# Shared experts' norms without a mean: centred down weights, routed rows centred on their way out of PSUM, variances in 32 rows

## The reference

```python
m = jnp.mean(x, axis=-1); v = jnp.var(x, axis=-1); norm = (x - m) / jnp.sqrt(v + 1e-5)
# 8 experts of 352 hidden features, the best 2 of them for each token
y = jnp.einsum('tef,te,ehf->th', act, combine, down_weights)
# shared expert of 704 hidden features, for every token
y = y + (silu(x @ gate.T) * (x @ up.T)) @ shared_down.T
x = norm(x + y)
```

## Time and profile before

| | us |
|---|---|
| median of 3 runs (2693.25 to 2711.85) | 2700.85 |
| the profiled execution, its own time | 2698.7 |
| its span in the profile | 2696.9 |
| TensorE busy in the span | 2416.9 (90%) |
| VectorE busy | 1855.0 (69%) |
| GpSimd busy | 1347.0 (50%) |
| ScalarE busy | 1281.6 (48%) |

### The profile page before, as it was taken

The page is one execution under the profiler, slowest core; times in us unless marked ns, Lnnn a source line. Parts: engine busy times, 40 slices in busy tenths (PEclk is TensorE's granted clock), DMA queues, the critical chain, the costliest instruction groups (busy, mean ns, idle before and its releaser), DMA issues.

```text
span 2696.9 us, 33625 instructions
## 1 busy us (share of the span) xinstructions
PE 2416.9 (90%) x11898; PEld 1391.1 (52%) x11898; DVE 1855.0 (69%) x2248; ACT 1281.6 (48%) x2059; POOL 1347.0 (50%) x610
## 2 busy tenths in 40 slices
PE   7887749999999999999488899999999988999998
PEld 2333324444677999865133333333433333678886
DVE  5768875544665666575799889889988988741222
ACT  4444335531234666443657656764675452234433
POOL 0222239850050000340699999999999995122221
PEclk9999869989899999999799899999999999999999
DMA  6464443332064777540464675666577555100000
GB/s 231 144 156 112 127 104 93 91 101 94 13 231 143 271 269 271 196 152 18 127 194 160 188 213 175 201 194 195 172 198 215 195 180 204 45 1 16 1 16 32
DMA packets 251641, 387.11 MB, mean 144 GB/s; under 512 B 131776, under 2 KB 154304, under 8 KB 243808
## 3 DMA queue, kind: packets, MB, share of 16 engines
q1 hardware_dynamic: 232016, 336.76, 38.5%
q0 software_dynamic: 9296, 38.80, 5.8%
q10 hardware_dynamic: 10176, 9.50, 1.0%
HBM read 315.00 MB, written 62.65 MB: 140 GB/s over the span
## 4 chain that ended last, share of the span: by engine, by line
PE 56%; DVE 13%; POOL 10%; issue 9%; DMA 5%; ACT 4%; SPq 2%; ACTq 0%; PEldq 0%; PEld 0%; POOLq 0%; DVEq 0%
PE psum L2143 8%; POOL arena L862 5%; PE psum L2090 5%; PE psum L2324 4%; PE psum L2325 4%; POOL arena L854 3%; DMA arena<-bc_scr 3%; PE psum L3235 2%; PE psum L3035 2%; DVE arena L2787 2%; SPq L2417 2%; PE psum L2297 2%; PE psum L1986 2%; PE psum L2298 2%; PE psum L1988 2%
## 5 line engine op out<-in xcount | busy, mean ns | idle before, releaser
L854 POOL TENSOR_TENSOR arena<-arena 128x2048 f32<-128x2048 f32 x128 | 600.8, 4694 | 111.0 <-DVE arena L1635 74.7
L2143 PE MATMUL psum<-arena,cst 128*128 128x512 f32 x1024 | 501.8, 625 | 92.9 <-POOL arena L862 83.1
L1162 ACT ACTIVATE psum<-arena,negA 128x512 f32<-128x512 f32 x512 | 333.4, 682 | 281.1 <-DVE arena L1650 240.4
L2143 PEld LDWEIGHTS psum<-arena,cst 128*128 128x128 f32 x1024 | 188.4, 195 | 385.6 <-issue 209.8
L1650 DVE TENSOR_TENSOR_SCAN arena<-psum,arena 128x512 f32<-128x512 f32 x256 | 310.8, 1214 | 101.6 <-POOL arena L854 58.8
L862 POOL TENSOR_TENSOR arena<-arena 128x1024 f32<-128x1024 f32 x128 | 323.3, 2526 | 19.3 <-DMA arena<-bc_scr 10.3
L1650 DVE TENSOR_TENSOR_SCAN psum<-psum,arena 128x512 f32<-128x512 f32 x256 | 296.9, 1205 | 0.1
L911 POOL TENSOR_TENSOR arena<-arena 128x512 f32<-128x512 f32 x64 | 87.1, 1361 | 324.8 <-ACT arena L1286 319.3
L2090 PE MATMUL psum<-arena 128*128 128x512 f32 x512 | 231.5, 596 | 1.3 <-PE psum L2090 0.8
L1770 DVE TENSOR_TENSOR r<-arena,r 128x512 fp32r<-128x512 f32 x64 | 46.1, 722 | 237.6 <-ACT r L1291 237.5
L2324 PE MATMUL psum<-r 128*128 128x512 f32 x512 | 201.5, 394 | 3.6 <-ACT arena L1286 2.5
(11 more groups left out here) (392 smaller groups left out, 4868.5 us busy)
## 6 DMA issues: line engine op xcount, KB each, us to landing
arena<-bc_scr SPq DMA_DIRECT2D x256, 512.0 KB, 4.8
arena<-w_exp SPq DMA_DIRECT2D x23, 1408.0 KB, 6.1
arena<-in_gu SPq DMA_DIRECT2D x44, 512.0 KB, 4.8
arena<-in_inw SPq DMA_DIRECT2D x32, 512.0 KB, 3.5
arena<-in_dn SPq DMA_DIRECT2D x31, 512.0 KB, 6.9
x_scr<-arena SPq DMA_DIRECT2D x19, 512.0 KB, 6.0
arena<-in_x SPq DMA_DIRECT2D x8, 1024.0 KB, 10.1
w_exp<-in_gu SPq DMA_DIRECT2D x16, 512.0 KB, 7.4
```

The lines of the kernel that those rows point to most:

```text
L854: nc.gpsimd.tensor_tensor(dB[:, at:at + 2], du[:, j:j + 2].unsqueeze(1).broadcast_to([P, 2, 2, T]), BR[:, q % 2].unsqueeze(2).broadcast_to ...
L1162: nc.scalar.activation(psum[:, bank], dt[:, b % 2, j + t], ACT.Exp, scale=negA2[:, at:at + 1]).then_inc(s["da_ok"], 1)
L2143: ins = mm(psum[:, t], ident, dB[:, k % NSLOT, t], start=False, stop=(n == NS - 1), skip_group_check=True)
```

## The change

A weight matrix whose columns have their mean over the output features taken away gives outputs whose mean is zero. The shared down weights are centred so: ScalarE reads each block once more with a sum along the row (`mean_down`), and VectorE's two splitting instructions add the result (a tensor_scalar in place of the cast, a scalar_tensor_tensor in place of the tensor_tensor). The routed rows are centred as they leave PSUM: `rows_out` becomes two ScalarE instructions, one that sums and one that copies with the sum as bias, with a wait between them. x itself has no mean after the norm ahead. So `mean_pe` and `center_dve` go for the four norms, the squares wait for x alone, the variances of batches 0 to 2 use `var_rows_pe`, and their spreading (with masks that GpSimd now also sets behind fetch(1)) stands behind the up products of the next step (19, 21, 23). The scaling of a batch moves to the end of that step. Batch 3's norm in the scan stage loses its mean and its centring.

```diff
+        sml = view(41984, 512, "p (n m) -> p n m", n=4)
...
         def square_act(act, q):
-            act.wait_ge(s["ln_c"], q + 1)
+            if B <= q < 2 * B:
+                act.wait_ge(s["x_ok"], q + 1)
+            else:
+                act.wait_ge(s["ln_c"], centred(q))
...
-        def spread_last_rows(pe, q):
+        def spread_last_rows(pe, q, masks):
...
             fetch(0)
             fetch(1)
+            nc.gpsimd.memset(sml, 0.0).then_inc(s["hs_ok"], 1)
+            wait(pool, "hs_ok", 4)
+            for n, r in enumerate(rowq):
+                nc.gpsimd.memset(sml[r, n], 1.0 / D).then_inc(s["hs_ok"], 1)
+                wait(pool, "hs_ok", 5 + n)
             add_rows(0)
...
+        def mean_down(act, n):
+
+            act.wait_ge(s[f"f_din{n % 4}"], 16 * loads(n))
+            if n == 0:
+                act.wait_ge(s["og_ok"], 4 * B)
+            if n == NA:
+                wait(act, "wl_ok", 4 * NBLK)
+            if n > NA:
+                act.wait_ge(s["f_du"], n - 1)
+            if n > 1:
+                wait(act, "mu_ok", n)
+            to = sink if 0 < n < NA else dnj[pair(n)]
+            nc.scalar.activation(to, dn[slot(n)], ACT.Identity, scale=-1.0 / D,
+                                 accum_out=small[:, 32 + n % 4:33 + n % 4]).then_inc(s["mu_ok"], 1)
...
-                cp(ob[:, k % 2, h - H0[k]], psum[:, 2 + h % 2]).then_inc(s["bo_ok"], 1)
+                nc.scalar.activation(ob[:, k % 2, h - H0[k]], psum[:, 2 + h % 2], ACT.Identity, scale=-1.0 / D,
+                                     accum_out=small[:, h % 4:h % 4 + 1]).then_inc(s["mc_ok"], 1)
+                wait(act, "mc_ok", h + 1)
+                nc.scalar.activation(ob[:, k % 2, h - H0[k]], psum[:, 2 + h % 2], ACT.Identity,
+                                     bias=small[:, h % 4:h % 4 + 1]).then_inc(s["bo_ok"], 1)
...
             for n in range(NA):
+                if n and n + 1 < NA:
+                    mean_down(act, n + 1)
                 silu(n)
                 if n == 0:
                     root_rows_act(act, B - 1)
+                    mean_down(act, 1)
...
             rows_out(NH - 1)
+            mean_down(act, NA)
             for n in range(NA, NS2):
                 silu(n)
                 round_h(n)
...
                 if part == 1:
-                    root_act(act, B + b)
+                    root_last(act, B + b)
+                if n + 1 < NS2:
+                    mean_down(act, n + 1)
                 if n == NA + 2:
                     round_x(3)
                 for i in combined(n + 1):
...
-                v.tensor_copy(dnh[pair(n)], dn[slot(n)]).then_inc(s["f_dh"], 1)
+                wait(dve, "mu_ok", n + 1)
+                less = small[:, 32 + n % 4:33 + n % 4]
+                v.tensor_scalar(dnh[pair(n)], dn[slot(n)], less, None, ALU.add).then_inc(s["f_dh"], 1)
                 dve.wait_ge(s["f_dh"], n + 1)
-                v.tensor_tensor(dnl[pair(n)], dn[slot(n)], dnh[pair(n)].bitcast(F32), ALU.subtract).then_inc(s["f_ds"], 1)
+                v.scalar_tensor_tensor(out=dnl[pair(n)], in0=dn[slot(n)], scalar=less, in1=dnh[pair(n)].bitcast(F32),
+                                       op0=ALU.add, op1=ALU.subtract).then_inc(s["f_ds"], 1)
...
                 b, part = norm_of(n)
-                if part == 0:
-                    center_dve(dve, B + b)
-                if part == 1 and n < NS2 - 2:
-                    scale_dve(dve, B + b)
+                if part == 1:
+                    reciprocal_last(dve, B + b)
+                if part == 0 and b:
+                    apply_last(dve, B + b - 1)
...
-            scale_dve(dve, 2 * B - 2)
+            apply_last(dve, 2 * B - 2)
             add_shared(B - 1)
...
                     if b == 0:
-                        if p == CENTER_FIRST:
-                            center_dve(dve, 2 * B - 1)
...
                 gate_or_up(n, 0)
-                if part == 0:
-                    pe.wait_ge(s["ln_std"], B + b)
-                    mean_pe(pe, B + b)
                 gate_or_up(n, 1)
+                if norm_of(n - 1)[1] == 1:
+                    wait(pe, "hs_ok", 8)
+                    spread_last_rows(pe, B + norm_of(n - 1)[0], sml)
                 if part == 1:
-                    var_pe(pe, B + b)
+                    pe.wait_ge(s["ln_done"], B + b)
+                    var_rows_pe(pe, B + b)
...
                     if b == 0:
-                        if p == MEAN_FIRST:
-                            mean_pe(pe, 2 * B - 1)
...
             nc.scalar.copy(xh[0], x[:, :, 0:T]).then_inc(s["xh_ok"], 1)
+            mean_down(act, 0)
             square_act(act, B - 1)
```

More of the change, by code:

```diff
@@ L119, in build @@
         dnh = [rview(at, D) for at in (41984, 42496, 37120, 37632)]
-        dnl = [rview(at, D) for at in (43008, 43520, 38144, 42496)]
+        DNL_AT = (43008, 43520, 38144, 42496)
+        dnl = [rview(at, D) for at in DNL_AT]
         hah = [rview(at, 512) for at in (44032, 44544, 45056, 45568)]
@@ L292, in build @@
                 ("pm_ok", "kc_ok", 2 * B), ("o_re", "g_ev", 4 * B), ("ob_mm", "g1_mm", 16 * B), ("ln_b", "pt_ok", B), ("hs_ok", "kc_mm", 2 * B),
+                ("mu_ok", "g_free", 2 + 8 * B), ("mc_ok", "bc_used", 4 + 4 * B),
                 ("w_in0", "m_in", 128 * B), ("w_in1", "t_out", 128 * B), ("xr_in0", "xload", 32 + 96),
@@ L340, in build @@
         dn = [view(at, D) for at in (29952, 30464, 30976, 31488, 32000, 32512)]
+        dnj = [view(at, D) for at in DNL_AT]
+        sink = tA[:, 1472:1472 + D]
         hs = [view(at, 512) for at in (36096, 36608, 43008, 43520)]
@@ L452, in ln_act, with centred @@
             root_act(act, q)
+        def centred(q):
+            return q + 1 if q < B else q + 1 - B
         def square_act(act, q):
-            act.wait_ge(s["ln_c"], q + 1)
+            if B <= q < 2 * B:
+                act.wait_ge(s["x_ok"], q + 1)
+            else:
+                act.wait_ge(s["ln_c"], centred(q))
             nc.scalar.activation(lnsq, x[:, :, (q % B) * T:(q % B + 1) * T], ACT.Square).then_inc(s["ln_sq"], 1)
@@ L468, in center_dve @@
             xb = x[:, :, (q % B) * T:(q % B + 1) * T]
-            dve.wait_ge(s["ln_mean"], q + 1)
+            dve.wait_ge(s["ln_mean"], centred(q))
             v.tensor_tensor(xb, xb, psum[:, 7].unsqueeze(1).broadcast_to([P, KT, T]), ALU.subtract).then_inc(s["ln_c"], 1)
@@ L504, in last_norm @@
         def last_norm(q):
-            return 4 * (B + 4 + q - (3 * B - 1))
+            return 4 * q
         def square_last(act, q):
             if q == 3 * B - 1:
-                act.wait_ge(s["ln_c"], q + 1)
+                act.wait_ge(s["ln_c"], centred(q))
             else:
@@ L518, in build @@
         smk = view(46336, 512, "p (n m) -> p n m", n=4)
-        def spread_last_rows(pe, q):
+        def spread_last_rows(pe, q, masks):
             pe.wait_ge(s["ln_c2"], q + 1)
             for n, t in enumerate(colq):
-                ins = nc.tensor.matmul(psum[:, 7, t], smk[:, n], lnrs[:, 0:P], start=True, stop=True)
+                ins = nc.tensor.matmul(psum[:, 7, t], masks[:, n], lnrs[:, 0:P], start=True, stop=True)
             ins.then_inc(s["ln_b"], 4)
@@ L638, in build @@
         NORM_AT = (3, 4, 6, 7, 8)
-        MEAN_FIRST, CENTER_FIRST, SQUARE_FIRST, VAR_FIRST = 10, 13, 14, 17
+        SQUARE_FIRST, VAR_FIRST = 14, 17
         ROOT_FIRST, INVERSE_FIRST, SPREAD_FIRST, SCALE_FIRST = 19, 20, 23, 25
@@ L900, in ternary_pool @@
             nc.gpsimd.memset(smk, 0.0).then_inc(s["hs_ok"], 1)
-            wait(pool, "hs_ok", 4)
+            wait(pool, "hs_ok", 9)
             for n, r in enumerate(rowq):
                 nc.gpsimd.memset(smk[r, n], 1.0 / D).then_inc(s["hs_ok"], 1)
-                wait(pool, "hs_ok", 5 + n)
+                wait(pool, "hs_ok", 10 + n)
             with pool.Fori(0, B * NC1 // 2) as h:
@@ L1671, in scale_tiles @@
                 if half == 0:
-                    wait(dve, "ln_b", 4 * (B + n + 2))
+                    wait(dve, "ln_b", 4 * (2 * B + n + 1))
                 xb = x[:, 2 * half:2 * half + 2, n % B * T:n % B * T + T]
@@ L2198, in spread_last @@
                     if q:
-                        wait(pe, "ln_b", 4 * (B + n + 1) + q)
+                        wait(pe, "ln_b", 4 * (2 * B + n) + q)
                     mm(psum[:, OUT_BANK, colq[q]], onesd[r, :], lnstd[r, 0:P], start=True, stop=True).then_inc(s["ln_b"], 1)
@@ L2329, in ternary_pe @@
                             if b == 0:
-                                wait(pe, "hs_ok", 8)
-                            spread_last_rows(pe, q)
+                                wait(pe, "hs_ok", 13)
+                            spread_last_rows(pe, q, smk)
                     if c >= 2:
```

## The result

Median of the changed kernel 2718.58 us (2704.34 to 2723.52, 13 runs), of the kernel before 2702.72 (2693.25 to 2711.85, 13 runs); ratio 1.0051, 95% interval 1.0037 to 1.0065. By the ratio that is 13.8 us slower (10.0 to 17.6 by its interval), too little to tell from no change by the 1% of the forecast, and 1.5 more than the +12.3 of the sum.

What follows compares the result with a forecast made beforehand. TensorE was taken as the bound in the routed and second shared stretches, VectorE in the scan. -18.5 + 2.4 + 5.8 + 16 + 5.4 + 3.3 - 2.1 = +12.3 on 2698.7 gave 2711 us, range 2686 to 2730.

Steps and rivals of the forecast that it cites:

- D: Routed stretch: the second instruction of `rows_out` adds a delay of 0.9 us in every half, costing 16 us (7 to 34).
- Rival 1: Routed stretch: ScalarE's second instruction is nearly hidden, delay 0.5 us or less, time 2702 to 2695 us; chance 0.20.
- rival 3: Routed stretch: the wait inside `rows_out` costs a full drain, delay 1.5 us, 34 us in all, time 2729; chance 0.12.
- E: First shared stretch, step 4: `mean_down` ahead of silu waits for weights, gate(5) starts 5.4 us later (3 to 7).
- F: Clock: TensorE runs at the low level behind the waits at step 4 and the fifth combine, 3.3 us (0 to 3.3).
- A: Second shared stretch, batches 0 to 2: six wide TensorE passes replaced by narrow ones, gain 18.5 us (17 to 20).
- B: First combine: GpSimd's add comes later through `rows_out` and the masks, TensorE loses 2.4 us (1.5 to 3).
- C: Fifth combine: `mean_down(16)` waits for `down(14)`, making scaling and fetch late; TensorE waits 5.8 us (3 to 8).
- Rival 2: Whole kernel: all waits vanish beside other work, only A and G are left, -20.6 us, time 2678; chance 0.08.
- G: Scan stage, batch 3's norm: a VectorE centring of 2.27 us goes, gain 2.1 us (0 to 2.5).
- Rival 4: Second shared stretch: splits become its bound if `mean_down` comes 3.5 us behind `down`, time 2717 us; chance 0.05.

Runs made afterwards that it cites:

- rows_copy: The changed kernel with the routed rows leaving PSUM by one plain copy, uncentred; ratio 0.9990 to the kernel before, routed stretch 270.2 us.
- mean_late: The changed kernel with the first shared stretch's down-row mean moved behind the rounding of activations; ratio 1.0021 to the kernel before.
- mean_free: The changed kernel with the second shared stretch's unused mean output written into the silu tile, without waiting for the down product; ratio 1.0025 to the kernel before.
- scale_first: The changed kernel with the scaling of routed rows put ahead of the mean in the second shared stretch; ratio 1.0087 to the kernel before.

## Why the prediction was right

Sum +12.3, measured +13.8; the time 2711 stands beside 2714.8 + 1.9 = 2716.7 of the profiled execution, which also holds the 4.1 us of the stage ahead, and in the range. The mechanisms came as told; that the total is off by only 1.5 is luck, as the end of this section shows. By steps:

- **D, +16 (7 to 34).** Measured +12.6 between the kernels, and 14.9 by `rows_copy`. The chain held as told, over the next weight piece, `lo` and `act_lo`, with 23 of 39 down products waiting. I had two of five halves losing 0.6 there, and a third losing 0.9 at the gate product behind `tokens_lo`. Three of five lose 0.53 at down, and the third only 0.09 more at that gate: 1.7 in five instead of 2.1. The sign given for it, 7.1 us a half, came out at 7.10. The delay was 0.81, not 0.9: the second instruction starts 0.04 behind the read and the next one 0.58 behind it. The estimate by the price that the Trainium skill gives (ScalarE: Activation LUTs, section What ACT_TABLE_LOAD costs), 0.9, is as near to this as my own. Rival 1 (hidden) fell with `rows_copy`, rival 3 (a full drain, 34 us) with the 1.30 us of the rows.
- **E, +5.4, with its share of F +7.0.** Measured +9.8. That is over my upper bound of 7 and its 1.6 of F. The step is right and was mis-sized in two terms: the weights were there at 782.96, which is 778.9 with the 4.1 us of the early shift taken off, where I took 777.7; and a table load of 1.28 stands between the mean and silu, which I hadn't looked for in the queue. 7.0 + 1.2 + 1.3 = 9.5. The low clock took 2.0 instead of 1.6 (tile_in(7) to gate(5) 5.5 us instead of 3.55). `mean_late` gave 7.1 back.
- **A, B, C and the rest of F: -18.5 + 2.4 + 5.8 + 1.6 = -8.7.** Measured -4.1. C's wait was 6.31 for 5.8, and the chain as told: `mean_free` took it away and 7.5 us of the stretch with it, 4.4 to 7.7 against the other profiles. But its terms were further off than their sum. Counted from the last down product, the additions of tiles 2 and 3 began 2.1 later than I worked out and took 5.15 instead of 2.8 to 3.0, so the third fetch came 10.1 later and not 5.7; and TensorE, held up at B, came 3.0 later itself, where I had it come on time. B's was 3.02 against 0.47, so 2.55 for 2.4; with the 1.17 and 1.24 of the two other profiles it is 0.7 to 0.8. Missing in the sum is the clock behind B's wait: the second combine follows the first by 4.85 us where it took 3.27, +1.6, which I gave only to C and E. The rest, some 3 us, are small waits that I counted at nothing: 0.52, 0.28, 0.94 and 1.22 for VectorE's additions, reciprocals and scalings. A's own -18.5 can't be read alone; with B, C, the clock behind both and the small waits taken out of the -4.1 it comes to -19.1, inside 17 to 20, but with the 3 us by which this stretch spreads that bounds it loosely. Rival 2, that such waits vanish, fell with the rows of B, C and E.
- **F.** Granted clock 0.50 and 0.51 behind E and C, as told, and 0.55 behind B. With that the traces bear out what the Trainium skill says of idle gaps (TensorE: Matmul & The Clock Gate, section Why this matters for your kernels).
- **G, -2.1 (0 to -2.5).** Measured -4.9 in the two profiles, -5.8 by the means of three and eleven; the scan without the centring spreads over 8.8 us, so the size stays open. Both lie outside my bounds, which took VectorE's one pass for the whole effect; what else the mean held up in the scan I haven't looked into.
- **Rival 4** did not come about: the splits waited for the mean, but TensorE for none of them. `scale_first` shows how close it was: 2.5 us later and it decides.

The errors of E, +2.8, and of the second stretch, +4.6, were mostly made up for by D, -3.4, and G, -2.8. Their sizes add up to 13.6, more than the whole forecast of +12.3, so it is luck that the sum came within 1.5.

## What to carry to other kernels

Work given to an idle engine is priced by what stands behind it in that engine's queue, not by its idle share: ScalarE was busy for 61% of the routed stretch, and 0.81 us more at one place in each half cost 10 to 15 us, while the same work one half later cost 2 to 4. Look at what a new instruction waits for before asking where to put it: the mean ahead of the weighing cost 4 to 8 us by its wait, behind it 9 us more than that, and without the wait almost nothing of this. And a wait on the bounding engine costs its length and, behind the long ones here, the clock. Compare the same stretch over several profiles before reading a difference of 2 or 3 us.

## What the runs showed of the hardware

- Behind a wait of 3.02 us TensorE was granted 0.55 over the next 3.2 us, at a price of 1.6 us; behind the 2.31 us of `mean_late` in step 4 it was 0.57 over 4 us; behind the 2.19 us at the first combine of `mean_free` it stayed at 1.00, as behind the 1.17 of `mean_late` there. First the window of `mean_free`, then that of `mean_late`:

```profile
1169.60:1177.60 8.00, 8.00 (x39) 6.57 (x38) 5.88 (x8) 1.74 (x3) 6.94 (x5) 1.00 0.34 101
```

```profile
784.20:788.20 4.00, 4.00 (x11) 3.14 (x12) 2.55 (x5) 1.71 (x4) 3.09 (x4) 0.57 1.03 418
```

- VectorE and GpSimd at work at the same time can each take longer. Two additions of 128x512 on GpSimd took 2.49 us and then 5.15 in the changed kernel, the second time beside several VectorE passes, one of them, of 128x2048, taking 2.79, and 2.28 elsewhere. Which of the two pays varies: beside the same pass the additions took 3.00 in `mean_late` (rows above).

```profile
1167.51 2.49 POOL L842 TENSOR_TENSOR arena<-arena 128x512 f32<-128x512 f32 x2
1175.96 5.15 POOL L842 TENSOR_TENSOR arena<-arena 128x512 f32<-128x512 f32 x2 [5.96 <-ACT arena L1021]
...
1177.18 2.79 DVE L1511 TENSOR_TENSOR r<-arena,r 128x2048 fp32r<-128x2048 f32 x1
```

  The Trainium skill (GPSIMD Engine Reference, section Key points) says that the two share their SBUF interfaces and contend where VectorE has two SBUF inputs, as this pass has; these rows agree.

- The stage ahead of the change, the same in all kernels but for one mean on ScalarE that TensorE doesn't wait for, ended anywhere from 718.0 to 727.2 us. A difference of two spans under 9 us says nothing until the stretches have been compared.
